# Cross-attention and feed-forward on one core: layernorm pieces spread over the loop, transposes of x moved to the accumulator's bank, a ring of four feed-forward banks, and three ReLUs on VectorE

## What is computed

```python
def layernorm(x):                                   # eps 1e-5
    return (x - mean(x)) / sqrt(var(x) + eps)
q = rmsnorm((layernorm(x) @ Wq).reshape(B, S, 16, 128), gq)
k = rmsnorm((ctx @ Wk).reshape(B, S, 16, 128), gk)
v = (ctx @ Wv).reshape(B, S, 16, 128)
x = x + (softmax(q @ k.T / sqrt(128)) @ v).reshape(B, S, 2048) @ Wo
h = relu(layernorm(x) @ ternary(W_fc).T) ** 2        # 1024 wide
x = x + rms_norm(h) @ ternary(W_proj).T
```

## Time and profile before

| | us |
|---|---|
| median of 3 runs (365.19 to 366.36) | 366.35 |
| the profiled execution | 365.14 |
| its span, first to last instruction | 363.0 |
| PE busy | 329.8 (91%) |
| DVE busy | 268.1 (74%) |
| ACT busy | 270.3 (74%) |
| POOL busy | 210.5 (58%) |
| chain that ended last, by engine | PE 58%, DVE 14%, POOL 11%, issue 8%, ACT 5% |

### The profile page before, as it was taken

The page is one execution under the profiler, slowest core; times in us unless marked ns, Lnnn a source line. Parts: engine busy times, 40 slices in busy tenths (PEclk is TensorE's granted clock), DMA queues, the critical chain, the costliest instruction groups (busy, mean ns, idle before and its releaser), DMA issues.

```text
span 363.0 us, 8006 instructions
## 1 busy us (share of the span) xinstructions
PE 329.8 (91%) x2602; PEld 315.7 (87%) x2602; DVE 268.1 (74%) x564; ACT 270.3 (74%) x1056; POOL 210.5 (58%) x304
## 2 busy tenths in 40 slices
PE   7789798899779998999999989999998988959975
PEld 7789698899669998999999989999998988847764
DVE  2558486987667877888888788988886865775572
ACT  2778586988658887888888878888887875636660
POOL 3776568656576656666666655666546642054461
PEclk9999999999989999999999999999999999998996
DMA  7941017000000000000000000000000000000011
GB/s 228 360 152 43 8 39 264 15 0 3 0 0 3 3 0 2 3 1 3 1 2 2 1 2 2 2 2 2 1 3 1 3 0 2 2 0 0 3 58 58
DMA packets 10393, 11.51 MB, mean 32 GB/s; under 512 B 753, under 2 KB 9969, under 8 KB 10225
## 3 DMA queue, kind: packets, MB, share of 16 engines
q1 hardware_dynamic: 10064, 11.01, 9.2%
q10 hardware_dynamic: 288, 0.00, 0.0%
HBM read 9.96 MB, written 1.05 MB: 30 GB/s over the span
## 4 chain that ended last, share of the span: by engine, by line
PE 58%; DVE 14%; POOL 11%; issue 8%; ACT 5%; DMA 2%; DVEq 0%; SPq 0%; POOLq 0%; ACTq 0%
PE bT L737 5%; POOL rr L375 3%; PE bA L649 3%; PE bA L647 3%; PE bA L648 3%; DVE PTl L972 3%; PE bT L714 3%; POOL xn L343 3%; PE bO L647 3%; DVE qn L988 3%; PE bY L647 3%; PE bT L705 3%; PE bO L649 3%; PE bO L648 3%; PE bY L649 2%
## 5 line engine op out<-in xcount | busy, mean ns | idle before, releaser
L380 POOL TENSOR_SCALAR Pr<-Pr,rs 128x256 f32<-128x256 f32 x128 | 65.4, 522 | 70.6 <-DVE rs L1018 70.5
L516 ACT ACTIVATE Pr<-bS,nb 128x256 f32<-128x256 f32 x128 | 59.2, 472 | 0.0
L375 POOL TENSOR_TENSOR rr<-sse,mhalf 128x8 f32<-128x8 f32 x31 | 51.6, 1666 | 2.6
L1011 DVE TENSOR_REDUCE nb<-bS 128x2 f32<-128x512 f32 x64 | 44.1, 690 | 8.8 <-PE bS L649 5.4
L524 ACT ACTIVATE PTh<-bT 128x512 fp32r<-128x512 f32 x64 | 39.2, 614 | 14.5 <-PE bT L737 14.4
L972 DVE TENSOR_TENSOR PTl<-bT,PTh 128x512 fp32r<-128x512 f32 x64 | 43.5, 680 | 2.7 <-ACT PTh L524 2.7
L647 PE MATMUL bY<-WWh,Oh 128*128 128x256 f32 x128 | 41.3, 323 | 1.3 <-DVE WWl L972 1.3
L647 PE MATMUL bO<-PTh,ch 128*128 128x256 f32 x128 | 39.1, 306 | 2.5 <-DVE PTl L972 2.1
L530 ACT ACTIVATE Oh<-bO 128x256 fp32r<-128x256 f32 x64 | 25.3, 396 | 21.4 <-PE bO L649 21.1
L972 DVE TENSOR_TENSOR Ol<-bO,Oh 128x256 fp32r<-128x256 f32 x64 | 26.8, 418 | 18.2 <-ACT Oh L530 18.2
L737 PE MATMUL bT<-ident,Pr 128*128 128x128 f32 x256 | 38.4, 272 | 0.0
(11 more groups left out here) (186 smaller groups left out, 1156.6 us busy)
## 6 DMA issues: line engine op xcount, KB each, us to landing
Wqr<-in_L_xattn_Wq SPq DMA_DIRECT2D x8, 256.0 KB, 3.6
Wor<-in_L_xattn_Wo SPq DMA_DIRECT2D x2, 1024.0 KB, 8.7
Wkr<-in_L_xattn_Wk SPq DMA_DIRECT2D x8, 128.0 KB, 2.8
Wvr<-in_L_xattn_Wv SPq DMA_DIRECT2D x1, 1024.0 KB, 7.2
WvT<-in_L_ffn_W_fc SPq DMA_DIRECT2D x1, 1024.0 KB, 7.0
Wor<-in_L_ffn_W_proj SPq DMA_DIRECT2D x1, 1024.0 KB, 8.9
out<-xn SPq DMA_DIRECT2D x4, 256.0 KB, 2.2
xt<-in_x SPq DMA_DIRECT2D x1, 768.0 KB, 9.5
```

Source lines behind the costliest of these rows:

```text
L375: gp.tensor_tensor(rr[:, :], sse[:, :], mhalf[:, 0:2 * UT], ALU.pow).then_inc(r_done, 1)
L380: last = gp.tensor_scalar(Pr[u][:, t, :], Pr[u][:, t, :], rs[u][:, t:t + 1], 1.0, ALU.mult, ALU.mult)
L516: last = act.activation(Pr[u][:, t, :], bS[u][:, t * SKV:(t + 1) * SKV], ACT.Exp, bias=nb[u][:, t:t + 1], scale=1.0, accum_out=su[u][:, t: ...
L1011: dve.tensor_reduce(nb[u][:, :], bS[u][:, :].rearrange("p (t k) -> p t k", t=QT), AX.X, ALU.max, negate=True).then_inc(nb_done[u], 1)
```

## The change

In the attention: `ln_norm` of GpSimd makes one tile a call, and the two tiles of a batch stand behind `norm_p(i+1, 0)` and behind `norm_p(i+1, 1)` (for batch 3 the second tile a loop later); `ln_rstd` stands ahead of them (`LN_AT`). `ctx_copy` and `ctx_low` go to other loops (`CTX_AT`). The turns of x move from loops 4, 6, 7, 12, 20, 28 and one in the feed-forward to loops 4, 8, 16, 24, 29 and two in the feed-forward. Those of loops 8, 16 and 24 go through bY, between the `residual` that empties it and the next batch's first `project`; `residual` moves ahead of `maxes(i+1, 1)`. The turns of the ternary weights (`turn_w`) and `up(0)`, `up(1)` move into loops 30 and 31.

In the feed-forward: the `up` blocks and the two banks of `sums_f` take turns in a ring of four (bB, bA, bT0, bT1); `up(m+4)` stands behind `down(m)` up to block 13, then `up(m+3)`. The last `sums_f` is split in three, of which one stands behind block 13. VectorE, not ScalarE, makes the ReLU of blocks 8, 11 and 14. `f2_done` is counted for each half. The normalising of batch 3 stands behind `hidden_lo(3)`.

```diff
...
...
-        hr_done = sem("hr_done")
+        hr_act = sem("hr_act")
+        hr_dve = sem("hr_dve")
...
-        f2_done = sem("f2_done")
+        f2_done = [sem("f2_done0"), sem("f2_done1")]
...
-        wt_banks = [bA, bB, bA, bB]
-        h_banks = [bA, bB, bT[0]]
+        wt_banks = [bB, bA, bB, bA]
         f_banks = [[bS[0], bS[1]], [bO, bY]]
-        fs_bank = bT[1]
-
-        X_CALLS = [(0, bT[0]), (1, bB), (2, bB), (3, bB), (0, bB), (1, bB), (2, bB), (3, bT[1])]
-        X_AT = {4: 2, 6: 3, 7: 4, 12: 5, 20: 6, 28: 7}
...
+        FS_AFTER = [13, 15]
+        turns = [bB, bA, bT[0], bT[1]]
+
+        def h_turn(m):
+            return m + sum(m > after for after in FS_AFTER)
+
+        def h_bank(m):
+            return turns[h_turn(m) % 4]
+
+        def fs_turn(g):
+            return h_turn(FS_AFTER[g]) + 1
+
+        def fs_bank(g):
+            return turns[fs_turn(g) % 4]
+
+
+        RELU_DVE = [m for m in range(2 * HT) if m % 3 == 2 and m > HT - 2]
...
+        X_CALLS = [(0, bT[0]), (1, bB), (2, bY), (3, bY), (0, bY), (1, bA), (2, bO), (3, bO)]
+        X_AT = {4: 2, 8: 3, 16: 4, 24: 5, 29: 6}
+
+
+        LN_AT = {2: (1, 2), 5: (2, 3), 6: (3, 4), 10: (0, 5), 18: (1, 6), 26: (2, 7)}
+
+        CTX_AT = {6: 1, 11: 2, 19: 3}
...
                 if i - 2 in T_AT:
                     ternary(T_AT[i - 2])
+                if i in LN_AT:
+                    ln_rstd(LN_AT[i][1], LN_AT[i][0])
                 if pair(i + 1):
                     norm_p(i + 1, 0)
                 if i + 4 < PAIRS:
                     split_q_hi(i + 4)
                     split_q_lo(i + 4)
+                if i in LN_AT and i > 2:
+                    ln_norm(*LN_AT[i], 0)
+                if i == 7:
+                    ln_norm(*LN_AT[6], 1)
                 if pair(i + 1):
                     norm_p(i + 1, 1)
-                if i == 2:
-                    ln_rstd(2, 1)
-                if i == 5:
-                    ln_rstd(3, 2)
-                    ln_norm(2, 3)
-                if i == 6:
-                    ln_rstd(4, 3)
-                    ln_norm(3, 4)
-                if 5 <= i < B + 4:
-                    ctx_low(i - 4)
-                if i > PAIRS and i % PAIRS == 2:
-                    ln_rstd(B + i // PAIRS, i // PAIRS - 1)
-                    ln_norm(i // PAIRS - 1, B + i // PAIRS)
+                if i in LN_AT and i > 2 and i != 6:
+                    ln_norm(*LN_AT[i], 1)
+                if i in CTX_AT:
+                    ctx_low(CTX_AT[i])
...
-                if m == HT + 2:
+                if m == HT + 3:
...
-                bank_ = h_banks[m % 3]
+                bank_ = h_bank(m)
                 act.wait_ge(hs_done, m + 1)
                 if g == 1:
-                    act.wait_ge(f2_done, j + 1)
-                elif j >= HT - 2:
+                    act.wait_ge(f2_done[1], j + 1)
+                else:
                     act.wait_ge(y_done, 2 * (STEPS - HT + 1 + j))
                 act.activation(sTh[:, j, :], bank_[:, :], ACT.Copy).then_inc(sh_done, 1)
...
+                if i == STEPS - 2:
+                    weights(2)
                 if pair(i):
                     p_hi(i, 1)
-                if i == STEPS - 1:
-                    weights(2)
                 if pair(i + 1):
                     exps(i + 1, 0)
-                if i == STEPS - 2:
-                    weights(0)
                 if i == 0:
                     ww_hi(5)
                 if pair(i):
                     o_hi(i, 0)
+                if i == STEPS - 1:
+                    relu(0)
...
-                if 5 <= i < B + 4:
-                    ctx_copy(i - 4)
-            relu(0)
+                if i == STEPS - 3:
+                    weights(0)
+                if i + 1 in CTX_AT:
+                    ctx_copy(CTX_AT[i + 1])
+            relu(1)
             o_hi(STEPS - 1, 1)
-            relu(1)
-            for m in range(2 * HT):
+            hidden(0)
+            relu(2)
+            for m in range(1, 2 * HT):
                 hidden(m)
-                if m + 2 < 2 * HT:
+                if m == 1:
+                    x_hi(7)
+                if m + 2 < 2 * HT and m + 2 not in RELU_DVE:
                     relu(m + 2)
-                if m == 3:
+                if m == 4:
...
-                if n - 3 in X_AT:
+                if n - 3 in X_AT and X_CALLS[X_AT[n - 3] - 1][1] is bB:
...
+                    pe.wait_ge(xl_done, b + 2)
...
                     pe.wait_ge(t_done, CHUNKS)
-                    pe.wait_ge(qn_done, STEPS)
+                    pe.wait_ge(kn_done, STEPS)
                 if n == 1:
-                    pe.wait_ge(kn_done, STEPS)
+                    pe.wait_ge(xl_done, 6)
...
+            def h_free(turn):
+                m = turn - 4 - sum(turn - 4 >= fs_turn(g) for g in range(2))
+                if turn - 4 == fs_turn(0):
+                    pe.wait_ge(fv_done, 1)
+                else:
+                    pe.wait_ge(sl_done, m + 1)
...
+            def up(m):
+                g, j = divmod(m, HT)
...
+                if m == 3:
+                    pe.wait_ge(ptl_done[1], STEPS)
+                if j == 0:
+                    pe.wait_ge(xl_done, B + 2 * (g + 1))
+                if m >= 4:
+                    h_free(h_turn(m))
...
+                if i == STEPS - 2:
+                    turn_w(1)
                 if pair(i):
                     turn_p(i, 0)
                 if pair(i - 1):
                     project(i - 1, 0)
+                if i == STEPS - 2:
+                    turn_w(2)
                 if pair(i + 1):
...
+                if i == STEPS - 2:
+                    turn_w(3)
+                    up(0)
                 if pair(i):
                     attend(i, 0)
+                if i == STEPS - 1:
+                    up(1)
                 if pair(i + 2):
                     turn_q(i + 2)
-                if i in X_AT:
+                if i == 4:
                     pe.wait_ge(kn_done, i + 3)
+                    turn_x(X_AT[i])
+                if i == STEPS - 3:
+                    pe.wait_ge(qn_done, STEPS)
+                    turn_x(X_AT[i])
+                if i in X_AT and i % PAIRS == 0:
+                    pe.wait_ge(x1_done, i // PAIRS)
                     turn_x(X_AT[i])
                 if pair(i + 3):
...
+                for half in range(2):
+                    for t in range(2):
...
+                    last.then_inc(f2_done[half], 1)
+
+            def sums_f(g, part, first, final):
...
+
             attend(STEPS - 1, 1)
-            up(1)
+            up(2)
             project(STEPS - 1, 0)
-            up(2)
+            up(3)
             project(STEPS - 1, 1)
+            pe.wait_ge(ol_done[1], STEPS)
+            turn_x(7)
             for m in range(2 * HT):
                 if m == 2 * HT - 1:
-                    sums_f(1)
+                    sums_f(1, h4[(2 * HT - 2) % 3], False, False)
+                    pe.wait_ge(h4_done, 2 * HT)
+                    sums_f(1, h4[(2 * HT - 1) % 3], False, True)
                 down(m)
-                if m + 3 < 2 * HT:
+                if m + 4 <= FS_AFTER[0]:
+                    up(m + 4)
+                if m == 3:
+                    pe.wait_ge(xl_done, 7)
+                    turn_x(8)
+                if m == FS_AFTER[0] - 3:
+                    h_free(fs_turn(0))
+                    pe.wait_ge(ha_done, HT)
+                    sums_f(0, ha[:, 0, :], True, True)
+                if FS_AFTER[0] - 3 < m < 2 * HT - 3:
                     up(m + 3)
-                if m == 2:
-                    turn_x(8)
-                if m == HT + 1:
-                    sums_f(0)
+                if m == 2 * HT - 3:
+                    h_free(fs_turn(1))
+                    pe.wait_ge(ha_done, 2 * HT - 2)
+                    sums_f(1, ha[:, 1, :], True, False)
 
...
+            def relu(m):
+                dve.wait_ge(f1_done, m + 1)
+                dve.wait_ge(hs_done, m - 1)
+                dve.tensor_scalar(hr[m % 2], h_bank(m)[:, :], 0.0, None, ALU.max).then_inc(hr_dve, 1)
+
+            def relu_square(m):
+                if m in RELU_DVE:
+                    dve.wait_ge(hr_dve, relus_dve[m])
+                else:
+                    dve.wait_ge(hr_act, relus_act[m])
+                u = h_bank(m)[:, :]
...
                     o_lo(i - 1, 1)
+                if i == STEPS - 2:
+                    weights(1)
...
                     q_norm(i + 2)
+                if i > 0 and i % PAIRS == 0:
+                    residual(i // PAIRS - 1)
...
                 if i in T_AT:
                     t_scale(T_AT[i])
+                if i == STEPS - 2:
+                    weights(3)
+                if i == STEPS - 1:
+                    relu_square(0)
                 if i == 1:
...
-            relu_square(0)
+
+            relu_square(1)
             o_lo(STEPS - 1, 1)
-            relu_square(1)
             hidden_lo(0)
             relu_square(2)
```

(102 more changed lines are left out.)

47 lines of the change are left out of this document (3 added, 44 removed).

## The result

The changed kernel takes 344.0 us (341.9 to 344.2, four runs) against 365.8 of the kernel before (364.3 to 366.4): a ratio of 0.940, 95% interval 0.935 to 0.945. 343 was forecast. The profiled execution took 344.1, its span is 342.0.

The account below looks back on a forecast made before the run. TensorE's own work, 8.20 us a loop, was taken as the bound, with stalls above it. Span 363.0 - 14.5 - 8.1 = 340.4, plus 2.1 outside is 342.5, raised to 343 us; range 339 to 350.5.

Parts of the forecast that it names:

- GpSimd's pieces: Loops 5, 6, 7, 10, 18, 26: layernorm tiles fit GpSimd's holes; with the turns, 14.5 us less, 0.5 paid for ctx_copy.
- The turns: Turns of x in loops 8, 16, 24: 0.5 us each, 1.5 in all, instead of 1.3 a time; loop 29 free.
- full clock from 20 us to the end: Sign expected in the profile after: TensorE at full clock from 20 us until the kernel's end.
- Loops 30 and 31: End of attention: weight turns and up(0), up(1) move into waits; taken at 0, between -1 and +1.5 us.
- The feed-forward: From attend(31, 1): chain spans three blocks, not two; 35.2 us work plus 3.2 waits; 8.1 us less including the end.
- The end: Behind the last sums_f at 349.4: mean, power and finish in a row, span's end at 354.9 us.
- The ReLUs: Feed-forward: three ReLUs on VectorE relieve ScalarE of 1.5 us, but neither is the bound, so worth nothing.
- The rival of half clock: Feed-forward: waits at down(3), down(4), up(8) bring half clock that pauses keep until the end; 375 us, chance 0.03.
- the 3.63: Feed-forward of the kernel before: TensorE's 3.63 us wait until 323.96, while VectorE normalises the last batch; half clock follows.

Follow-up runs that it names:

- the two runs in bB: Changed kernel with the turns of x in loops 8, 16 and 24 made in bB: 349.2 us; that kernel with residual put back behind o_lo(i, 0): 349.4 us.
- the last run: Changed kernel with later ternary work, the last layernorm's power behind the third sum of squares, and all ReLUs on ScalarE: 338.9 us.

## Why the prediction was right, step by step

The forecast span was 340.4, the measured one 342.0. By stage, after minus before:

| | forecast | measured |
|---|---|---|
| up to `q_norm` of pair 7 | 0 | +0.9 |
| pairs 7 to 31 | -14.5 | -14.7 |
| pair 31 to the last attend | 0 (-1 to +1.5) | +0.5 |
| behind it | -8.1 | -7.8 |
| sum | -22.6 | -21.1 |

**GpSimd's pieces.** Right, in place and size. Putting them back cost 8.03 us by the loops. No tile was stretched: the ten took 1.21 to 1.23 each, the same as before. The Trainium skill ("SBUF — State Buffer", "Who interferes with whom") says that a VectorE instruction with two SBUF inputs contends with a GpSimd one that reads SBUF. These tiles hardly try it: a ternary comparison of VectorE overlapped only those of loops 6 and 7 at 93.49 and 101.69 us, by their last 0.15 us.

**The turns.** 0.44 each, against 0.5. `ctx_copy` cost 0.18 in each of three loops (pairs 7, 12 and 20 at 8.38; pairs 8 and 28, with a layernorm but without it, at 8.19 and 8.20), 0.5 as taken. The forecast had the gain as a turn's own price of 1.3 before; in the loops of `residual` the alternative cost 1.83, which only the two runs in bB showed.

**The start.** No step had it. The wait of ScalarE for W_fc was in the trace before, where TensorE waits 2.1 us for it in loop 3, and the prediction took everything ahead of pair 7 as unchanged. The +0.9 is two terms, -1.0 and +1.9. The opening up to pair 4 was 1.0 shorter than in the one profile of the kernel before; it differs by 1.1 us between profiles of the changed kernel's family too. Pairs 4 and 5 took 18.7 us before, 20.6 in the changed kernel and 23.1 in its repetition, by the length of the wait and by the half clock behind it. The run that moves the ternary work shows the cause: 16.4, no wait and no half clock. The kernel before has the same wait; what that edit would give there was not run. So the sign "full clock from 20 us to the end" did not hold.

**Loops 30 and 31.** +0.5, inside the -1 to +1.5 that was stated. The waits there are 1.02 ahead of `attend(30, 1)` and 0.54 ahead of `turn_k`.

**The feed-forward.** The mechanism was right: the chain of `up`, `relu`, `hidden`, `hidden_lo`, `down`, divided by the blocks that `up` runs ahead, was shown by the run with `up` three ahead. Two terms were mis-sized against each other. A block is 1.87, not 1.97: the `down` of the earlier trace rows that was read as 1.03 held about 0.1 of handover. From the last attend to the end of `down(15)` it was 38.6 us, against 38.4 summed; with 4.2 of waits, counted as what each `down` came later than 1.87 and its sums and turns explain, the work was 34.4 and not 35.2. The waits were 4.2, not 3.2 (the parts that the prediction names add up to 3.05): 1.7 at `down(3)` for 1.05, 0.5 each at `down(4)` and `down(5)` for 0.8 and 0.7, 0.4 and 0.5 at `down(13)` and `down(14)`. That the two errors nearly cancel is luck. `hidden(3)` did wait for the power on GpSimd and the first copy, 2.53 us by the row at 309.14. With that power moved, `down(3)` came 1.6 us sooner and 0.95 us was kept.

**The end.** The sum has mean, power and finish in a row, and gives no reason why `finish` no longer waits for `down(15)`. In the kernel before it did: the first `finish` starts at 358.78, released by the matmuls into bY the earlier trace rows, though the power had ended at 358.05, and `down(15)` ran at half clock. In the changed kernel it starts behind the power, 0.03 us after it, since `f2_done` is counted for each half of the rows. From the start of `down(15)` to the end of the span it is 5.7 us for 6.4. So up to 0.7 of the 7.8 us comes from that small edit or from the clock there; no run has it by itself.

**The ReLUs.** Worth nothing, as taken.

**The rival of half clock** did not come: the stretch from 67.6 to 340 us ran at full clock, the wait of 1.53 and the smaller ones in it. The pauses of which the Trainium skill warns ("TensorE: Matmul & The Clock Gate", "A second HAM failure mode: psum-queue depth-cycling") had no such effect with a ring of four here. The prediction's reading that the kernel before had half clock only behind the 3.63 left out the stretch from 356.2 us to its end.

## What to carry to other kernels

When an engine's in-order program has holes in every loop, measure them and cut occasional work to their size: nothing got faster on GpSimd here, and 8 of 21 us came from that, by the run with the layernorm in one piece. Count how many blocks the producer runs ahead, not how many buffers there are, and check which passes of the other engines stand between a bank's filling and its emptying, since all of them are in its chain. An engine with room to spare needs no relief, and a wait for a transfer that looks constant in one trace should be looked up in a second.

## What was not expected of the hardware

The length of TensorE's wait in loop 3 does not tell how much half clock follows. In the kernel before, none followed a wait of 2.1 us:

```profile
64.50 0.39 PE L647 MATMUL bO<-PTh,ch 128*128 128x256 f32 x1 [2.06 <-DVE PTl L972]
```

In all nine profiles of the changed kernel's family that have this wait, half clock followed: 3.4 us of it after waits of 1.75 (layernorm in one piece), 2.4 (the changed kernel) and 3.95 (`up` three ahead), but 6.8 after 3.65 (turns in bB) and 4.0 (the repetition). The change alone does not decide it: two executions of the changed kernel without a profile had a mean granted clock of 0.998 and 0.999, which leaves room for less than 2 us at the half level, and the kernel before ran at means from 0.970 to 0.994.

Half clock also began during the last sums, matmuls with a single column, with TensorE shown as busy: at 356.2 us in the kernel before, at 335.8 in the run with the later power, where it cost 0.8 of a saving of 1.0, and at 331.9 in the last run. Why it came early in some and after the last matmul in others was not settled.
